# When the next expert's weights are cast and split, and when the last batch is routed, in a fused attention and mixture-of-experts kernel

## The reference

```python
def _moe(x, Wgate, expert_bias, Wg, Wu, Wd, sWg, sWu, sWd):
    xf = x.reshape(-1, c)
    shared = jnp.mean(_experts(xf, sWg, sWu, sWd), axis=1)      # one shared expert, every token
    logits = xf @ Wgate + expert_bias
    probs = jax.nn.softmax(logits, axis=-1)
    topk_p, topk_i = jax.lax.top_k(probs, 2)                    # 2 of 8 experts for each token
    topk_p = topk_p / jnp.sum(topk_p, axis=-1, keepdims=True)
    ...
    routed = jnp.einsum('ne,nec->nc', comb, _experts(xf, Wg, Wu, Wd))
    return (shared + routed).reshape(b, t, c)
```

## Time and profile before

| | |
|---|---|
| median of 3 runs | 2330.65 us (2325.38 to 2334.54) |
| the profiled execution | 2325.74 us, its span 2324.0 us, 1.74 us lie around it |
| mean granted TensorE clock | 0.964 |
| PE busy | 2103.3 us, 91% of the span |
| DVE, ACT, POOL busy | 64%, 51%, 59% |
| issue of store b, b = 0 to 7 (L1878) | 1813.24, 1838.54, 1861.48, 1881.53, 1906.25, 1925.53, 1944.72, 1975.19 us |
| last matmul of the shared stage begins | 1963.06 us |
| first matmul of the expert stage | 1976.68 us |

### The profile page before, as it was taken

How to read it: one execution, slowest core, us unless ns; L and a number is a source line. 1 busy time by engine, 2 the same in 40 slices (tenths; PEclk the granted TensorE clock), 3 DMA queues, 4 the chain that set the end, 5 groups by cost and what they waited for, 6 DMA issues and landing times. The chain is left out here.

```text
span 2324.0 us, 43302 instructions
## 1 busy us (share of the span) xinstructions
PE 2103.3 (91%) x12568; PEld 958.9 (41%) x12569; DVE 1489.1 (64%) x4180; ACT 1180.0 (51%) x2319; POOL 1374.2 (59%) x1450
## 2 busy tenths in 40 slices
PE   2899999999999977799999999999984897899997
PEld 1333333333333312344444444544432443455554
DVE  3688888888888874466566565655544678344443
ACT  3355555555555544345545455554544673455554
POOL 4267776776776765255656565665661575455554
PEclk7999999999999987899999999999997998999999
DMA  5513323232332222534535354353514676666665
GB/s 161 168 55 110 101 85 103 81 115 73 107 97 92 78 98 86 170 115 139 159 118 153 117 163 134 114 174 98 155 49 159 120 156 126 114 116 112 115 109 91
DMA packets 227973, 272.15 MB, mean 117 GB/s; under 512 B 40152, under 2 KB 165964, under 8 KB 227508
## 3 DMA queue, kind: packets, MB, share of 16 engines
q1 hardware_dynamic: 197324, 212.76, 30.3%
q0 software_dynamic: 22752, 47.86, 12.1%
q10 hardware_dynamic: 7704, 9.20, 1.2%
HBM read 161.82 MB, written 86.54 MB: 107 GB/s over the span
## 5 line engine op out<-in xcount | busy, mean ns | idle before, releaser
L501 ACT ACTIVATE a_pt<-a_bank 128x512 f32<-128x512 f32 x512 | 305.6, 597 | 370.2 <-DVE a_bank L608 367.3
L1439 DVE CUSTOM_DVE_ANT_0 b_bank<-b_bank,b_tri 128x256 f32<-128x256 f32 (+3 forms) x512 | 253.2, 497 | 296.0 <-PE b_bank L1579 291.8
L619 DVE CUSTOM_DVE_ANT_0 a_bank<-a_bank,a_strip 128x512 f32<-128x512 f32 x512 | 353.2, 691 | 4.6 <-PE a_bank L762 3.9
L1192 POOL TENSOR_TENSOR b_acc<-b_acc,b_pt 128x256 f32<-128x256 f32 (+2 forms) x384 | 279.2, 749 | 84.2 <-ACT b_pt L1305 73.3
L411 POOL TENSOR_TENSOR a_acc<-a_acc,a_pt 128x512 f32<-128x512 f32 x256 | 317.5, 1271 | 16.2 <-ACT a_pt L501 15.7
L608 DVE TENSOR_TENSOR a_bank<-a_bank,a_band 128x256 f32<-128x256 f32 (+1 forms) x512 | 205.6, 402 | 129.7 <-PE a_bank L749 128.5
L1305 ACT ACTIVATE b_pt<-b_bank 128x256 f32<-128x256 f32 (+2 forms) x384 | 143.7, 383 | 187.1 <-PE b_bank L1563 171.1
L749 PE MATMUL a_bank<-a_q_stack,a_k_stack 128*128 128x512 f16 x512 | 199.2, 390 | 22.9 <-ACT a_pt L501 13.9
L762 PE MATMUL a_bank<-a_k_stack,a_q_stack 97*128 97x512 f16 x512 | 196.4, 384 | 3.6 <-DVE a_low L619 3.5
L1964 POOL DMA_INDIRECT out_dram<-c_z,c_to_row x71 | 112.5, 1585 | 133.8 <-DMA out_dram<-c_z,c_to_row 97.6
L1578 PE MATMUL b_bank<-b_k_stack,b_q_stack 96*128 96x256 f16 (+3 forms) x512 | 154.6, 302 | 16.0 <-DVE b_low L1439 8.7
(11 more groups left out here) (338 smaller groups left out, 5352.7 us busy)
## 6 DMA issues: line engine op xcount, KB each, us to landing
b_q_stack<-qk_rows SPq DMA_DIRECT2D x192, 128.0 KB, 2.6
a_q_stack<-qk_rows SPq DMA_DIRECT2D x96, 128.0 KB
a_k_stack<-qk_rows SPq DMA_DIRECT2D x96, 128.0 KB
b_k_stack<-qk_rows SPq DMA_DIRECT2D x96, 128.0 KB, 2.6
a_sums<-in_x SPq DMA_DIRECT2D x34, 256.0 KB, 3.2
qk_rows<-a_qk_hi SPq DMA_DIRECT2D x64, 128.0 KB, 1.7
qk_rows<-a_qk_lo SPq DMA_DIRECT2D x64, 128.0 KB, 1.8
out_dram<-a_sums SPq DMA_DIRECT2D x32, 256.0 KB, 2.0
```

What stands on the lines that cost most here:

```text
L501: nc.scalar.activation(pt[:, n % SLOTS, :], st_bank[n % 2][:], ACT.Exp).then_inc(exped, 1)
L619: nc.vector.tensor_tensor_reduce(out=max_bank[step % 2][:], in0=max_bank[step % 2][:], in1=strip[:, g * HG + hh, at:at + S], scale=-1.0, s ...
L1192: nc.gpsimd.tensor_tensor(sums_of, sums_of, probs(n), ALU.add).then_inc(pooled, 1)
L1439: nc.vector.tensor_tensor_reduce(out=max_bank[step % 2][:, 0:w], in0=max_bank[step % 2][:, 0:w], in1=tri[:, at:at + w], scale=-1.0, scalar ...
```

## The change

SP's instructions stay as they are. On **ACT** the cast of expert b+1 is cut in two: gate and up in iteration b between the second and the third `high`, down after the second `hidden_high`; `scale_gate` moves behind them. On **DVE** the split moves from iteration b+1 into iteration b: gate and up between the two `activate`s, down ahead of `finish_rows`. In the last iteration but one (b = 6) the routing of batch 7 is finished (`choose` and `settle`) ahead of `finish_rows`; PE's `route` and `rank` and ACT's `exponential` are moved to match, and POOL may scatter the last batch's records one iteration earlier. In the last iteration the block table is made first of all, and three `set_from_row` come ahead of the last `finish_rows`. PE's first transposes of the expert stage no longer wait for all weights.

```diff
             def scatter_some(b, n):
-                for _ in range(min(n, left[0] - (B - 1 - b) * NT)):
+                known = B if b >= B - 2 else b + 1
+                for _ in range(min(n, left[0] - (B - known) * NT)):
...
             normalise(0)
-            weights(0)
+            up_weights(0)
+            down_weights(0)
...
                 if more:
                     high(b + 1, 0)
                     high(b + 1, 1)
-                    scale_gate(b + 1, range(0, 2))
+                up_weights(b + 1)
+                if more:
                     high(b + 1, 2)
                     high(b + 1, 3)
                 hidden_high(b, 0)
...
                 squash(b, 1)
                 if more:
-                    scale_gate(b + 1, range(2, 4))
+                    scale_gate(b + 1, range(0, 2))
+                if b + 2 == B:
+                    exponential(b + 1)
                 hidden_high(b, 1)
+                down_weights(b + 1)
                 if b + 2 < B:
                     normalise(b + 2)
+                    exponential(b + 1)
                 if more:
-                    exponential(b + 1)
-                weights(b + 1)
+                    scale_gate(b + 1, range(2, 4))
...
+            for b in range(B):
+                more, early = b + 1 < B, b + 2 == B
                 if more:
+                    settle(b)
+                    if b == 0:
+                        find_spare()
                     low(b + 1, 0)
                     low(b + 1, 1)
                 else:
                     lay_starts()
+                    lay_blocks()
                 activate(b, 0)
...
-                if b:
-                    up_weights(b)
+                up_weights(b + 1)
+                if early:
+                    choose(b + 1)
                 activate(b, 1)
-                if not more:
+                if early:
+                    settle(b + 1)
+                elif more:
+                    choose(b + 1)
+                else:
                     low_part(1)
-                    lay_blocks()
-                if more:
-                    choose(b + 1)
-                if b:
-                    down_weights(b)
+                    set_from_row(Count(0, 0, 4))
+                    set_from_row(Count(0, 1, 4))
+                    set_from_row(Count(0, 2, 4))
+                down_weights(b + 1)
                 for t in range(NT):
                     finish_rows(b, t)
-            up_weights(B)
-            down_weights(B)
...
-            pe.wait_ge(w_split, PARTS * X)
-            pe.wait_ge(out_done, TT)
             pe.wait_ge(table_ready, 1)
...
                     x_turn(x_in[:, 0], 0, 0)
+                    pe.wait_ge(w_split, PARTS * X)
+                    pe.wait_ge(out_done, TT)
```

More of the change, by code:

```diff
@@ L1926, in _ @@
                     add_to_output(b - 1)
-                write_records(b)
                 if b + 1 == B:
@@ L1930, in _ @@
                     continue
+                write_records(b)
                 if b > 1:
@@ L1938, in _ @@
                 low_part(b, 1)
+                if b + 2 == B:
+                    write_records(b + 1)
                 if b:
@@ L2010, in scale_gate, with up_weights @@
                     nc.scalar.activation(z[:, b % 4, t, :], z[:, b % 4, t, :], ACT.Copy, scale=gate[:, 1:2]).then_inc(gated, 1)
-            def weights(e):
+            def up_weights(e):
                 act.wait_ge(gu_loaded, 32 * (e + 1))
@@ L2015, in weights, with down_weights @@
                     nc.scalar.activation(gu_hi[:, e * NK + k, :], gu_stage[:, k, :], ACT.Copy, scale=wn[:, 1, k:k + 1]).then_inc(w_hi_done, 1)
+            def down_weights(e):
                 act.wait_ge(d_loaded, 16 * (e + 1))
@@ L2307, in _, with set_from_row, settle @@
             choose(0)
-            for b in range(B):
-                more = b + 1 < B
+            def set_from_row(at):
+                dve.wait_ge(entered[at.slot], at.use * 16 + 32)
+                v.tensor_copy(from_row[:, at.slot, :], entry[:, bass.ds(at.n, 1), 0]).then_inc(from_set, 1)
+            def settle(b):
                 shares(b)
@@ L2344, in x_low @@
                                 ALU.subtract).then_inc(x_lo_done, 1)
-            def set_from_row(at):
-                dve.wait_ge(entered[at.slot], at.use * 16 + 32)
-                v.tensor_copy(from_row[:, at.slot, :], entry[:, bass.ds(at.n, 1), 0]).then_inc(from_set, 1)
             def set_to_row(at):
@@ L2353, in set_to_row @@
                 v.tensor_copy(to_row[:, at.slot, :], entry[:, bass.ds(at.n, 1), 1]).then_inc(to_set, 1)
-            for j in range(4):
-                set_from_row(Count(0, j, 4))
+            set_from_row(Count(0, 3, 4))
             def step(at):
@@ L2469, in _ @@
                 up(b, 1, 0)
+                if early:
+                    route(b + 1)
                 up(b, 1, 1)
-                if more:
+                if more and not early:
                     route(b + 1)
@@ L2474, in _ @@
                     down(b, t, (0,))
+                if early:
+                    rank(b + 1)
                 for t in range(NT - 1):
```

2 lines of the change are left out of this document (removed).

## The result

| | before | after |
|---|---|---|
| median | 2328.3 us (4 runs, 2325.38 to 2334.54) | 2389.82 us (4 runs, 2387.63 to 2392.22) |
| profiled execution, span | 2324.0 us | 2387.0 us |
| mean granted TensorE clock | 0.964 | 0.955 |

The ratio is 1.0261 (95% interval 1.0235 to 1.0286): slower by 2.6%. The forecast was 2385 us in a range of 2362 to 2405.

A forecast was written before the change was run, and what follows sets the result against it. PE's work was taken as the floor, about 19 us an iteration, with weights landing about 21 us behind the opening store in iterations 1 to 4. 19.3 + 43.6 + 2 - 8 + 2 = +59 us on 2325.74: 2385 us, range 2362 to 2405.

The forecast's parts named there:

- start of the third pass and iteration 0: Iteration 0: expert 1's cast and split come into idle time and cost nothing; without that cover at most 3.3 us, once.
- iteration 1: ACT's earlier cast waits 20 us for expert 2's weights with batch 2's tiles queued behind; store 1 goes out 19.3 us later.
- iterations 2 to 4: Store, loads, cast and next store close a loop; three rounds take 111.3 us instead of 67.7, +43.6 us.
- +2 for the clock: Iterations 1 to 4: PE returns from stops at a lower clock; 2 us in all, 6 as the bound.
- iterations 5 to 7, up to the last sums: Casts wait for nothing; batch 7's routing delays iteration 6 and is gone from 7: +2 us, between 0 and +4.2.
- seam, last sums to steady work: From DVE's last sums to PE's steady work: 15.8 us instead of 23.8, -8 us; bounds 0 and -13.2.
- a round of 37.1 us: Iterations 2 to 4, store to store: store lands 11.5, z and weights 9.6, cast 2.5, chain 8.3, four scatters 5.2.
- ACT's waits were to be 15 to 20 us: Sign of being right: ACT idles that long ahead of the first c_gu_hi cast in iterations 1 to 4, none in 5 to 7.
- The waits vanish: Rival: weights of experts 2 to 5 are in the stage when ACT comes; iterations 2 to 4 take 57.6 us, 2304 us; chance 0.05.
- The loop turns faster: Rival: with less DMA traffic a round takes 34.9 us, 2373 us, or 2369 by the skill's 6.15 us; chance 0.20.
- Slower: Rival: a 14.0 us store, 10.8 us load and slow PE each round, no seam gain: 2408 us; chance 0.17.
- Cancel: Rival: gains and losses cancel within 0.5% (12 us of 2330.65), with stalls of some 16 us in all; chance 0.03.

The follow-up runs named there:

- e1: The changed kernel with SP's loads of the next expert's weights moved ahead of the load of z: 2319.94 us, ratio 0.996 to the kernel before.
- e6: The changed kernel with batch 7's routing, block table and conversions as before, only the weights' casts and splits moved: 2381.2 us, ratio 1.0225 to the kernel before.
- e5: The changed kernel with the stores of batches 0 to 3 adding only half of their rows: 2373.65 us, ratio 1.0195 to the kernel before.
- e9: The changed kernel with weights loaded ahead of z and batch 7's shares (settle) behind batch 6's sums, its records scattered an iteration later: median 2319.0 us.
- e11: The changed kernel with weights ahead of z, batch 7's shares behind the sums, and pick, exponential and rank moved behind batch 6's work: median 2317.8 us.

## Why the prediction was right, point by point

| term | forecast | measured |
|---|---|---|
| start of the third pass and iteration 0 | 0 | +1.2 |
| iteration 1 | +19.3 | +17.9 |
| iterations 2 to 4 | +43.6, and +2 for the clock | +44.3 |
| iterations 5 to 7, up to the last sums | +2 | +5.6 |
| seam, last sums to steady work | -8 | -8.0 |
| expert stage behind it | 0 | +2.1 |
| sum | +59 | +63 |

The measured column compares the two profiled executions (2388.86 and 2325.74 us); the medians differ by 61.5. The first +1.2 lies almost wholly ahead of the shared stage, and the first two rows belong together: store 1 was forecast for 1857.8 and went out at 1857.61.

**Iterations 1 to 4** are shown: ACT waits for the DMA ahead of four casts and none later, e1 takes the loss away by SP's order alone, e6 has it without the routing, and e5 shortens it by shortening the store. Of a round of 37.1 us the parts were off in ways that cancel. From store to cast it took 20.2, 19.3 and 20.0 us where I summed 21.1, 3.8 us less in three rounds. From the cast to the next store it took 18.6, 17.0 and 17.0 instead of 16.0, 4.6 us more. That the total came within 1 us of the forecast is in that part luck. Of the 4.6 us the sums, late on a slow PE, account for the 2.31 and 0.76 us that POOL waits ahead of stores 2 and 4; I had booked 2 us for the clock, with 6 as the bound. The second group of `down` products of iterations 2, 3 and 4 shows it:

```profile
1888.99 0.58 PE L2459 MATMUL c_bank<-c_d_hi,c_h_hi 128*128 128x512 f16 x1 [1.76 <-POOL c_h_lo L1882]
...
1926.78 0.38 PE L2459 MATMUL c_bank<-c_d_hi,c_h_hi 128*128 128x512 f16 x1 [1.75 <-POOL c_h_lo L1882]
...
1963.80 0.58 PE L2459 MATMUL c_bank<-c_d_hi,c_h_hi 128*128 128x512 f16 x1 [1.75 <-POOL c_h_lo L1882]
```

In iteration 3 the group runs at full speed, and POOL does not wait ahead of store 3. The rest lies in the chain and in POOL's issues. The Trainium skill (TensorE: Matmul & The Clock Gate, "HAM oscillation") lets the penalty be paid in every round; the trace agrees that PE comes back slow each time (0.58 to 0.59 us for the first `down` matmul behind `route`, 0.38 when busy), but only some 3 us in three rounds reached the store, since POOL's scatters lay beside it. One sign was off: ACT's waits were to be 15 to 20 us, and that of iteration 2 was 21.05.

**Iteration 0** cost nothing, as said (from SP's first row of the third pass to store 0 it took 54.71 us where it took 54.57).

**The mis-sized term** is the step "In iteration 6 the routing of batch 7 comes ahead of the sums ... I take +2 us". I counted the 4.2 us of the shares on DVE and bounded the step by them, at +4.2. The pick, ACT's exponential and PE's rank product were moved too, and they stand ahead of batch 6's second hidden half and of its last `down` products; e9 against e11 shows that they hold iteration 6 without the shares. Iteration 6 grew by 4.8 us, and iteration 5 by 0.6; from store 6 to the last sums, where I let the same work be gone, nothing came back (+0.2). So the step measured +5.6, outside its bounds, and the sign that stores 4 to 6 lie 19 to 21 us apart held for iteration 5 (19.9) and not for 6 (24.0).

**The seam** came out at -8.0 as summed: 0.3 us to the store, 10.3 to the fourth gather, 5.2 to steady work.

**The expert stage** was not touched, but it does not start alike, and my sum had no term for that. Before, PE stops for 3.38 us ahead of its first `down` product and goes on at full speed (0.39 us); after, it stops for 8.33 us and comes back at the lower level of its clock (0.61 us, shown at the seam above). From 1990.84 and from 2051.80 the same instructions bring it to these rows:

```profile
1992.79 0.38 PE L2496 MATMUL c_bank<-c_gu_lo,c_xt_hi 128*128 x1
```

```profile
2055.44 0.38 PE L2515 MATMUL c_bank<-c_gu_lo,c_xt_hi 128*128 x1
```

That is 1.95 us before and 3.64 after. So the slow clock takes 1.7 of the 2.1 us, and of the 8.0 us that the seam gained 6.3 are kept. The stage takes 321.7 us from its first to its last `down` product before, 323.8 after, and 323.1 to 326.3 in the experiments; the other 0.4 us I take for variation between executions, which is argued, not shown.

**The rivals.** "The waits vanish" is what e1 shows when the order on SP is changed, and not without (and at 2319.94 us, not 2304). "The loop turns faster" is ruled out as a whole: the rounds took 38.8, 36.2 and 37.0 us, not 34.9. Its argument of less traffic beside the store did not hold either, as the last section shows. The 6.15 us for 1 MB that the Trainium skill states (DMA: Bandwidth & Descriptors, "Bandwidth") are measured on a transfer into SBUF and leave out the time of issuing, so the prediction's estimate did not compare like with like. The trace is not far from it for a load (the fastest 1 MB load of `z`, issued by SP, landed in 5.4 us here). No store of 1 MB landed under 9.4 us here, or under 9.2 in any run; all of them accumulate, so that this is the reason, as the prediction has it, is not shown. "Slower" needed stores of 14 us; behind the first, these took about 10.8 to the load of `z`. "Cancel" is out by the ratio; its bound of some 16 us of stalls goes by the median of 2330.65, while by the prediction's own base of 2325.74 it would be 21, which changes nothing.

## What to carry to other kernels

When an engine's work on a loaded tile is moved forward, find first when the tile lands, and what stands ahead of its load on the issuing queue: a load that must wait for a store holds every load behind it, and a consumer moved ahead of that landing turns the delay into a loop. Change the order of the loads together with the order of the work, or don't change either. When a chain of small steps over several engines is moved ahead, price it by what stands behind it on each of these engines, since each of them alone can hold the same result.

## What the runs showed of the hardware

Halving the accumulating store from 1 MB to 0.5 MB took only 2.4 to 3.8 us off the time until the load that waits for it (10.7 to 13.8 us before). Estimated from these two sizes, some 4 to 6 us of it don't shrink with the size. The store is slow although hardly anything lies beside it, in either kernel: between stores 1, 2 and 3 of the changed kernel and the loads of `z` that wait for them the DMA engines moved 97 to 100 GB/s, 1.06 to 1.08 MB in 10.7 to 10.9 us, and before, behind stores 1 and 2, 94 and 96 GB/s, 1.08 and 1.13 MB in 11.4 and 11.8 us; the store's own 1 MB is 1.05 of these. So whether a store would land later beside other traffic these runs can't say. A load of `z`, of the same 1 MB, landed within 5.6 us of its issue at the fastest (kernel before):

```profile
DMA to landing us min/median/max: 5.6/6.9/12.2
```

Only store 0 has something small beside it, the blank write of 16 KB, which makes 1040 packets; it took 14.0 us to the load of `z` before and 13.8 after, the longest of these. That the small packets are the cause is not shown.
